# Last group of a fused normalise-MLP-modulate kernel: variance by token, last product chunk by chunk, and the orders of groups 0 and 1 redone

## What is computed

```python
# x: 8 x 1024 tokens of 512 features
h = LN(LN(x, pw_g[id], pw_b[id]), cp_g[kind], cp_b[kind])   # two layer norms, rows looked up by token
t = LN(x, tm_g[kind], tm_b[kind]);  s = LN(x, ms_g[scale], ms_b[scale])
m, n, r = (x + LN(silu(c @ W1 + b1) @ W2 + b2) for each of three conditions)   # one row per batch
w = softmax(aw)
cat = [w0*h, w1*t, w2*m, w3*n, w4*r, w5*s]
u = silu(cat @ int_W1 + int_b1) @ int_W2 + int_b2
x1 = x + (u - mean(u)) / sqrt(var(u) + EPS) * int_g + int_be
style = cond @ (affine_w / 16).T + affine_b
dcoef = 1 / sqrt(sum((weight * style)**2) + 1e-8)
out = x1 + clip(((x1 * style) @ weight.T) * dcoef + bias, -256, 256)
```

## Time and profile before

| | us |
|---|---|
| runs | 1206.86 median of 3 (1206.23 to 1208.74) |
| the profiled execution's own time | 1205.75 |
| its span, first to last instruction | 1204.0 |
| PE, DVE, ACT, POOL busy | 1168.7, 945.9, 548.6, 228.5 |
| mean granted TensorE clock | 0.994 of full speed |

### The profile page before, as it was taken

How to read it: one execution, slowest core, us unless ns; L and a number is a source line. 1 busy time by engine, 2 the same in 40 slices (tenths; PEclk the granted TensorE clock), 3 DMA queues, 4 the chain that set the end, 5 groups by cost and what they waited for, 6 DMA issues and landing times.

```text
span 1204.0 us, 15227 instructions
## 1 busy us (share of the span) xinstructions
PE 1168.7 (97%) x5268; PEld 947.9 (79%) x5268; DVE 945.9 (79%) x1755; ACT 548.6 (46%) x849; POOL 228.5 (19%) x268
## 2 busy tenths in 40 slices
PE   5899899999999999999999999999999999999996
PEld 3567688888888888888888888888888888888884
DVE  7897887968788786878878688797878879687736
ACT  3546244453634446363453635345363444536352
POOL 3521211202121121112103111210212112021000
PEclk9999899999999999999999999999999999999998
DMA  9941231412333142233313223231323314122001
GB/s 320 347 159 42 70 121 43 142 59 88 103 97 120 36 140 69 79 112 96 112 35 124 77 86 121 70 131 42 105 86 97 120 43 142 60 88 88 27 1 69
DMA packets 52011, 119.50 MB, mean 99 GB/s; under 512 B 6464, under 2 KB 6848, under 8 KB 51840
## 3 DMA queue, kind: packets, MB, share of 16 engines
q1 hardware_dynamic: 36512, 67.58, 17.7%
q0 software_dynamic: 14336, 50.34, 12.7%
q10 hardware_dynamic: 1088, 0.62, 0.2%
HBM read 101.74 MB, written 16.78 MB: 98 GB/s over the span
## 4 chain that ended last, share of the span: by engine, by line
PE 91%; DVE 4%; DMA 2%; issue 1%; SPq 1%; POOL 1%; ACT 1%; DVEq 0%; ACTq 0%
PE pre L1152 14%; PE pre L1156 13%; PE pre L1159 13%; PE pre L1190 5%; PE pre L1192 5%; PE pre L1191 5%; PE uy L1210 5%; PE uy L1211 5%; PE uy L1213 5%; PE uy L1226 5%; PE uy L1223 5%; PE uy L1224 5%; PE turn L1131 2%; PE turn L1115 2%; DMA early_hi_l<-affine_t 2%; PE pre L1173 1%
## 5 line engine op out<-in xcount | busy, mean ns | idle before, releaser
L369 POOL DMA_INDIRECT gb<-pw_table,pw_ids x63 | 66.3, 1053 | 332.6 <-PE turn L1115 317.8
L1223 PE MATMUL uy<-hi_a,w_hi_l 128*128 128x512 f32 x256 | 100.5, 392 | 4.7 <-ACT hi_a L532 4.7
L1210 PE MATMUL uy<-hi_c,w_hi_w 128*128 128x512 f32 x256 | 101.4, 396 | 0.0
L1226 PE MATMUL uy<-lo_a,w_hi_l 128*128 128x512 f32 x256 | 100.6, 393 | 0.7 <-DVE lo_a L848 0.7
L1224 PE MATMUL uy<-hi_a,w_lo_l 128*128 128x512 f32 x256 | 100.3, 392 | 0.0
L1211 PE MATMUL uy<-hi_c,w_lo_w 128*128 128x512 f32 x256 | 100.0, 391 | 0.0
L1213 PE MATMUL uy<-lo_c,w_hi_w 128*128 128x512 f32 x256 | 99.9, 390 | 0.0
L1190 PE MATMUL pre<-hi_b,w_hi_x 128*128 128x512 f32 x256 | 99.8, 390 | 0.0
L1192 PE MATMUL pre<-lo_b,w_hi_x 128*128 128x512 f32 x256 | 99.7, 389 | 0.0
L1191 PE MATMUL pre<-hi_b,w_lo_x 128*128 128x512 f32 x256 | 99.6, 389 | 0.0
L387 POOL TENSOR_TENSOR ra<-vea,half 128x1 f32<-128x1 f32 x64 | 42.5, 664 | 281.3 <-DVE vea L745 281.3
(11 more groups left out here) (218 smaller groups left out, 2893.7 us busy)
## 6 DMA issues: line engine op xcount, KB each, us to landing
xT<-x_turned SPq DMA_DIRECT2D x64, 256.0 KB, 2.8
out_turned<-xT SPq DMA_DIRECT2D x64, 256.0 KB, 2.1
xt<-x_in SPq DMA_DIRECT2D x62, 256.0 KB, 2.6
sel_in<-sel_ids SPq DMA_DIRECT2D x16, 192.0 KB, 2.4
raw_s<-int_w SPq DMA_DIRECT2D x2, 512.0 KB
raw_h<-int_w SPq DMA_DIRECT2D x1, 1024.0 KB, 23.2
early_hi_w<-mlp_w SPq DMA_DIRECT2D x1, 1024.0 KB, 19.8
raw_w<-mlp_w SPq DMA_DIRECT2D x1, 1024.0 KB, 22.0
```

What stands on the lines that cost most here:

```text
L1210: pe.matmul(bank, w_hi["w2"][:, c, cut], hi["c"][:, c, :], start=c == 0, stop=False)
L1223: pe.matmul(bank, w_hi["l1"][:, c, cut], hi["a"][:, c, :], start=c == 0, stop=False)
L1226: last = pe.matmul(bank, w_hi["l1"][:, c, cut], lo["a"][:, c, :], start=False, stop=c == C - 1)
```

## The change

Four things change.

1. **Last group, root.** `last_variance` takes the sum over partitions with the squares as weights and a single column of 1/512 as moving operand: four matmuls in plain float32, one for each 128 tokens, with 128 x 1 results. DVE copies the 128 x 4 numbers, POOL takes the power, DVE writes four diagonal matrices (`last_diag`), and `spread_root`, one float32 matmul, spreads them to 128 x 512 in `turn`, where `make_x1` reads them. `split_sum`, `low_sum`, `read_var` and `find_root` are gone for group 15.
2. **Last group, product.** `last_y` writes to the four banks `pre` and goes chunk by chunk: outputs 0, 1, 2 together, then output 3. Its operands lie in ring c. Each `split_x1` of ACT comes between the `y_out` of group 14, and three `finish` of group 14 come behind `all_x1(15)`.
3. **Group 1.** The lo part of l1 is made by DVE in four chunks around group 1's first `low_t`, the hi part by ACT in four chunks around `hidden(0, 3)`; POOL's operation is gone. `find_root(0)` moves behind `second_norm(7)`.
4. **Group 0.** On ACT `split_h(0, 1)` comes ahead of the h weights, `gate(3)` and `split_h(0, 3)` ahead of all four `split_x`. POOL does `rstd_a(2)` and `rstd_a(3)` ahead of the h weights and the power `c_rs` between them, not behind four gathers. DVE takes `first_norm(2)` ahead of `make_s(0, 3)`, `second_norm(2)` ahead of the MLP's copy, all `low_h` ahead of all `low_x`, and the scaling `cT_ready` ahead of the second part of `wsum`; the softmax pieces are interleaved differently.

```diff
+    return uses + [("var", GROUPS - 1), ("root", GROUPS - 1)]
...
             rstd_a(1)
+            rstd_a(2)
+            rstd_a(3)
             low_h_weights(0)
             low_h_weights(1)
-            rstd_a(2)
+            pool.wait_ge(c_var, 1)
+            nc.gpsimd.tensor_tensor(crow[0:TROWS, 3:4], crow[0:TROWS, 2:3], half[0:TROWS, :], ALU.pow).then_inc(c_rs, 1)
             low_h_weights(2)
             low_h_weights(3)
-            rstd_a(3)
...
+            pool.wait_ge(var_read, GROUPS)
+            nc.gpsimd.tensor_tensor(last_root, last_var, half[:].to_broadcast([P, TPG]), ALU.pow).then_inc(last_rstd, 1)
...
             hidden(0, 2)
             filled(act, "batch")
             nc.scalar.activation(mh, filled(act, "dsum"), ACT.Copy).then_inc(dsum_copied, 1)
+            for c in range(2):
+                nc.scalar.activation(w_hi["l1"][:, c, :], raw_w["l1"][:, c, :], ACT.Copy).then_inc(hi_done["l1"], 1)
             hidden(0, 3)
+            for c in range(2, C):
+                nc.scalar.activation(w_hi["l1"][:, c, :], raw_w["l1"][:, c, :], ACT.Copy).then_inc(hi_done["l1"], 1)
...
             u_out(i, 3)
-            split_sum(i)
             y_out(i - 1, 0)
             y_out(i - 1, 1)
-            read_var(i)
+            split_x1(i, 0)
+            split_x1(i, 1)
             y_out(i - 1, 2)
+            split_x1(i, 2)
             y_out(i - 1, 3)
-            for c in range(C):
-                split_x1(i, c)
+            split_x1(i, 3)
...
             low_h(0, 2)
-            low_x(0, 0)
-            low_x(0, 1)
+            low_h(0, 3)
+            dve.wait_ge(style_ready, 1)
+            style4 = style[:].unsqueeze(2).to_broadcast([P, C, 4, BATCH])
+            nc.vector.tensor_tensor(sstyle.rearrange("p c (r b) -> p c r b", b=BATCH), style4, style4, ALU.mult).then_inc(style_ready, 1)
             dve.wait_ge(mlp2_mm, 1)
...
-            low_h(0, 3)
-            low_x(0, 2)
-            low_x(0, 3)
+            for c in range(C):
+                low_x(0, c)
             dve.wait_ge(c_rs, 1)
...
             make_t(1, 0)
+            low("l1", 0, 1.0)
             low_t(1, 0)
+            low("l1", 1, 1.0)
             add_square(0, 1)
...
+            bank = filled(dve, "var", i)
+            nc.vector.tensor_copy(last_var, bank[:, 0:TPG]).then_inc(var_read, 1)
             finish(i - 1, 0)
-            find_root(i)
-            finish(i - 1, 1)
+            dve.wait_ge(last_rstd, 1)
+            nc.vector.scalar_tensor_tensor(out=last_diag, in0=ident.unsqueeze(1).to_broadcast([P, TPG, P]), scalar=float(D),
+                                           in1=last_root.unsqueeze(2).to_broadcast([P, TPG, P]), op0=ALU.mult,
+                                           op1=ALU.mult).then_inc(last_scaled, 1)
             all_x1(i)
...
+            def last_variance():
+                bank = fill("var", GROUPS - 1)
+                pe.wait_ge(sq_added, 3 * GROUPS)
+                for j in range(TPG):
+                    last = pe.matmul(bank[:, j:j + 1], sq0[:, j * P:(j + 1) * P], vmat[:, 0:1].bitcast(F32), start=True, stop=True)
+                last.then_inc(turn_filled, 1)
...
             unit_y(i - 1, 0)
-            variance(i)
-            for o in range(1, C):
-                unit_y(i - 1, o)
-            for o in range(C):
-                unit_y(i, o)
+            last_variance()
+            unit_y(i - 1, 1)
+            spread_root()
+            unit_y(i - 1, 2)
+            unit_y(i - 1, 3)
+            pe.wait_ge(hid_raw, GROUPS * C)
+            last_y((0, 1, 2))
+            last_y((3,))
```

More of the change, by code:

```diff
@@ L554, in _ @@
             table_high("t")
-            act.wait_ge(aw_ready, 1)
+            split_rows(0)
+            act.wait_ge(aw_ready, 2)
             high("t", 0, wsm[:, 1:2])
-            split_rows(0)
             high("t", 1, wsm[:, 1:2])
@@ L589, in _ @@
             gate(2)
+            gate(3)
             split_h(0, 2)
+            split_h(0, 3)
             split_x(0, 0)
             split_x(0, 1)
-            gate(3)
-            split_h(0, 3)
             split_x(0, 2)
@@ L839, in make_x1 @@
                 dve.wait_ge(uy_read, u_use(i, c) + 1)
-                dve.wait_ge(root_ready, i + 1)
-                nc.vector.tensor_tensor(ug[:, c, :], ug[:, c, :], root[:], ALU.mult).then_inc(xq_done, 1)
+                if i + 1 < GROUPS:
+                    dve.wait_ge(root_ready, i + 1)
+                    rstd = root[:]
+                else:
+                    rstd = filled(dve, "root", i)
+                nc.vector.tensor_tensor(ug[:, c, :], ug[:, c, :], rstd, ALU.mult).then_inc(xq_done, 1)
                 dve.wait_ge(xq_done, i * C + c + 1)
@@ L890, in _ @@
             low_rows(0)
+            dve.wait_ge(aw_ready, 2)
             make_t(0, 0)
@@ L919, in _ @@
             low_h(0, 0)
-            make_s(0, 3)
             low("s", 2, wsm[:, 5:6])
             low_s(0, 2)
+            first_norm(2)
+            make_s(0, 3)
             low("s", 3, wsm[:, 5:6])
             low_s(0, 3)
-            first_norm(2)
+            second_norm(2)
             bank = filled(dve, "mlp_h").rearrange("p (c r) -> p c r", c=C)
@@ L1012, in _ @@
             make_t(1, 0)
+            low("l1", 0, 1.0)
             low_t(1, 0)
+            low("l1", 1, 1.0)
             add_square(0, 1)
             make_t(1, 1)
+            low("l1", 2, 1.0)
             low_t(1, 1)
@@ L1020, in _ @@
             make_t(1, 2)
+            low("l1", 3, 1.0)
             for i in range(1, GROUPS):
@@ L1041, in _ @@
                     dve.wait_ge(dco_ready, 1)
-                find_root(i - 1)
+                else:
+                    find_root(i - 1)
                 low_h(i, 1)
@@ L1049, in _ @@
                 second_norm(f - 1)
+                if i == 1:
+                    find_root(0)
                 low_h(i, 3)
@@ L1227, in unit_y, with spread_root, last_y @@
                 last.then_inc(y_ready, 1)
+            def last_variance():
[4 more added lines that the diff above has]
+                last.then_inc(turn_filled, 1)
+            def spread_root():
+                bank = fill("root", GROUPS - 1)
+                pe.wait_ge(last_scaled, 1)
+                pe.matmul(bank, vmat[:, 0:1].bitcast(F32).to_broadcast([P, P]), last_diag.rearrange("p j t -> p (j t)"),
+                          start=True, stop=True).then_inc(turn_filled, 1)
+            def last_y(outs):
+                i = GROUPS - 1
+                ring = x1_ring(i)
+                for c in range(C):
+                    pe.wait_ge(x1_hi, i * C + c + 1)
+                    for o in outs:
+                        pe.matmul(pre[:, o, :], w_hi["l1"][:, c, o * P:(o + 1) * P], hi[ring][:, c, :], start=c == 0, stop=False)
+                    for o in outs:
+                        pe.matmul(pre[:, o, :], w_lo["l1"][:, c, o * P:(o + 1) * P], hi[ring][:, c, :], start=False, stop=False)
+                    pe.wait_ge(x1_lo, i * C + c + 1)
+                    for o in outs:
+                        last = pe.matmul(pre[:, o, :], w_hi["l1"][:, c, o * P:(o + 1) * P], lo[ring][:, c, :], start=False, stop=c == C - 1)
+                        if c == C - 1:
+                            last.then_inc(y_ready, 1)
             def mlp_first():
```

67 lines of the change are left out of this document (30 added, 37 removed).

## The result

The changed kernel takes 1192.03 us, the median of 4 runs (1191.81 to 1192.47), beside 1206.55 (1204.79 to 1208.74) for the kernel before on the same chip: a ratio of 0.9877 with a 95% interval of 0.9861 to 0.9893. The forecast was 1192.1. The profiled execution took 1191.81, its span is 1189.7 against 1204.0.

The account below looks back on a forecast made before the run. PE, busy 97% of the span, was taken to bound the kernel, with DVE pacing part of group 0. End -7.8, group 1 -7.2, group 0 +0.2: -14.8 on the median 1206.86 gave 1192.1, range 1189.2 to 1196.0.

Parts of the forecast that it names:

- The end, -7.8 forecast: From `unit_y(14)` to the program's end: PE never waits, last matmul starts at 1191.2 against 1199.05; with 0.1 allowed, -7.8 us.
- The price of one column: End, `last_variance`: four float32 matmuls with one moving column take 0.81 us, as with 32 columns; bounds 0 and 3.4.
- The slack at `spread_root`: End: copy, power and DVE work of about 2.2 us fit into 2.7 us, half a microsecond of slack at best.
- The backlog of 0.1: Behind the last matmul: `y_out` and `finish` of outputs 0 to 2 come due together; 0.1 us allowed.
- Group 1, -7.2 forecast: Group 1: removing the 4.98 us stall and low clock's 2.6, less a 0.4 PE wait, gains 7.2 us.
- l1's parts on DVE at 0: Group 1: four new lo parts, 2.6 us on DVE, cost 0 because DVE waited there for ACT; uncovered, 2.6.
- Group 0, +0.2 forecast: Group 0: DVE's last three operations up to `c_ready` start 0.6 later, an idle 0.41 downstream goes; group's end +0.2 us.
- the full 0.90 for each of the two: Group 0: DVE loses 0.90 us beside each of two `low_h_weights` and 0.56 for POOL's small table, 2.36 in all.
- the upper bound of +1.5: Group 0: DVE waits for POOL's whole 3.10 and 0.56 us, moving the group's end by +1.5.
- the 2.4 us of group 0 that cost no clock: Group 0's old gate wait, cited in the late root rival as a pause as long as its 2.5 us.
- the rival of the late root: End: root's chain 3 us late, `spread_root` holds PE 2.5 us: 1194.6; chance 0.13, of which 0.03 at 1199.
- the time above the one before that had a chance of 0.02: Whole kernel: the case that the change makes it slower than before; chance 0.02.

Follow-up runs that it names:

- e3: Kernel before with only the change's new orders of group 0: 1206.39 us, ratio 0.9989 to the kernel before.
- e2: Kernel before with only the change's group 1 (l1's lo part on DVE, `find_root(0)` moved): 1199.81 us, ratio 0.9919.
- e7: Changed kernel with `find_root(0)` back in its old place, l1's lo part still on DVE: 1192.61 us, ratio 0.9881.
- e8: Changed kernel with l1's lo part back on POOL, `find_root(0)` in its new place: 1192.87 us, ratio 0.9882.
- e12: Changed kernel with one more, unused DVE operation ahead of each of the four lo parts of l1: 1193.14 us.
- e4: The changed kernel unaltered, run again beside the single parts: 1193.33 us, ratio 0.9861 to the kernel before.
- e11: The changed kernel unaltered, run again in a later call: 1192.25 us, ratio 0.9873 to the kernel before.
- e1: Kernel before with only the change's end (last group's root and product): 1197.30 us, ratio 0.9899.
- e9: Changed kernel with all of group 0 in its old order: 1191.66 us, ratio 0.986 to the kernel before.
- e5: Changed kernel with POOL's h weights and small table all ahead of the wait for `c_var`, then the power: 1190.01 us, ratio 0.9862.
- e10: The kernel of e5 run once more, in the same call as e11: 1188.85 us, ratio 0.984.

## Why the prediction was right, point by point

- **The end, -7.8 forecast, -7.70 measured.** The mechanism is as forecast. The price of one column, taken from the row of 32 columns, was exact: 0.81. The eight weight loads of the four matmuls take 1.08 with one column in the changed kernel (from 1163.93) and 1.09 with 32 columns in the kernel before (from 79.55). `spread_root` was 0.86, exact too. The rest is a pace of (23.39 - 1.67) / 95 = 0.229 us a matmul for the 0.226 that I read. The slack at `spread_root`, said to be half a microsecond at best, is 0.58. The backlog of 0.1 behind the last matmul is not there. The -7.70 holds against the trace of before; against the old ends of e3 and e2 it would be 1 to 2 us more.
- **Group 1, -7.2 forecast, -7.29 measured.** PE's wait at the lo matmuls is 0.17 instead of 0.4. What I hadn't seen is that the two edits overlap: e7 and e8 show that each removes most of the stall, so that they are no sum of two terms.
- **l1's parts on DVE at 0.** Right, and the traces show it apart: from `gain(t, 1, 0)` to the s gain that stood at 121.31, behind all four parts, PE takes 121.31 - 95.19 = 26.12 before, 26.08 in the changed kernel, and 122.64 - 96.50 = 26.14 in e8, where the parts are back on POOL. In e12 it is 27.04: of what was put in on top, 2.7, the cover takes 1.8 and 0.9 is left to pay.
- **Group 0, +0.2 forecast, +0.69 measured: the step that failed.** The prediction took "the full 0.90 for each of the two" `low_h_weights` and "0.56 again for the table", and had `low_x` stretched to 1.5 each. Both are wrong. POOL's power stands ahead of the weights in POOL's order and was itself held until the four `low_x` were through, so the weights never ran beside the `low_x`. Those weren't touched, and what they were to lose fell on one operation behind them: 3.72 - 0.60 = 3.12 for the 2.36 of the sum. The last operation up to `c_ready`, before and after:

```profile
60.71 0.69 DVE L953 TENSOR_TENSOR sq<-sq,xT 96x512 f32<-96x512 f32 x1
...
61.77 0.69 DVE L966 TENSOR_TENSOR sq<-sq,xT 96x512 f32<-96x512 f32 x1
```

  `c_ready` moved from 61.40 to 62.46, +1.06 where I had +0.6. From there to the gain row it is 33.42 for 33.79, about the idle 0.41 that I had taken out. PE's transpose did not move back: it stood at 63.35 before and stands at 62.61.

  The +0.69 is too small by luck. In all seven traces with the new orders and POOL's order of the changed kernel (after, e3, e4, e7, e8, e11, e12) the gain row comes 49.6 behind the start of `mlp_second`, and that start was 46.28 where the trace of before has 47.01. With the start of before the gain row would stand at 96.6: +1.4, about the upper bound of +1.5.

  The fault was to read the 0.43 and 0.90 of the earlier trace rows as a price for each pair of operations. There DVE and POOL took turns: POOL's two operations last 1.43 and 1.72, the second from 47.83, and each DVE operation was held only by what was left of the one POOL operation already begun. In the changed kernel DVE was let in only after all three.

  Which DVE operations POOL held up is shown one by one. Held up were the first of e8's two `lo_b`, with both operands in SBUF (1.63, where the second takes 0.68), and also two that read one SBUF tensor each, the operation of 3.72 and the integer step of the earlier trace rows, 4.74. Not held up was e8's operation of 0.69, with one operand in PSUM. So two operands in SBUF are not what all of them share; what decides it, no run shows.
- **The clock.** The prediction used "the 2.4 us of group 0 that cost no clock" as evidence that a pause so long is harmless. It held in the profiled execution of before, and e1, e2 and e9 show a fall behind pauses of 2.7 to 2.9. Behind the 1.9 us wait at the transpose the clock fell in e3, e4, e8 and e11 (0.56, 0.50, 0.61 and 0.50 in the lowest 3 us), and not in the changed kernel, e7 and e12. In these seven it cost nothing: the gain row comes 49.6 behind `mlp_second` with the fall and without, since DVE sets the pace there (busy for 31.91 to 31.98 of the 33.80 us from 61.30 to 95.10). So the clock is no rival for the gain of e5 and e10 either. The forecast didn't rest on it, but the rival of the late root did. At the end PE sets the pace, so 1194.6 may have been too mild a price for a pause of 2.5; no run tests it. Nor does a run show the time above the one before that had a chance of 0.02: where the clock fell behind the transpose, its mean from 61.30 to 95.10 was still 0.95 (e3, e4, e8, e11).
- **The total.** -14.8 against the profiled execution; it measured -14.3 in span and -14.5 in medians. In the two profiled executions the misses (+0.1 at the end, -0.1 in group 1, +0.5 in group 0) add up to 0.5. The median lies 0.1 from the forecast, and that closeness is partly luck: group 0 would have missed by 1.2 with the start of `mlp_second` as before, and that start moves the time about one for one (45.93, 46.28 and 48.58 in e11, the changed kernel and e4, whose profiled executions took 1191.26, 1191.81 and 1194.03). What carries the prediction are its two large terms.

## What to carry to other kernels

When DVE operations of the kinds held up here stand beside POOL's, count as the upper bound POOL's whole unbroken queue against the next DVE operation (3.72 for 0.60 here), and DVE's against POOL's (2.73 for the power's 0.59); one turn of the other engine is the lower one, as in the earlier trace rows (1.17 and 1.64 for 0.74). A POOL operation that someone waits for (here a power of one column) belongs at the end of such a queue, with the bulk work ahead of it in time that nobody needs: here two lines moved, 2.6 to 3.4 us and the fastest version of the study (1188.85). And before adding up two remedies for one stall, ask whether either alone removes it.

## What the runs showed of the hardware that was new to me

DVE and POOL did not meet only at semaphores: in the cases below no semaphore stands between the operation that was held up and those that held it. Unbroken runs of operations were mostly not interleaved: DVE's four `low_x` of 2.48 us held off a POOL power until they were through (2.73), and POOL's three operations of 3.5 us held off one DVE operation that asked 0.06 us after the first had begun (3.72), and about the same in e3, e4, e7, e8, e11 and e12. In the earlier trace rows a pair of POOL operations and two DVE operations did alternate: POOL's pair took 3.10 where it takes 2.50 alone (from 47.92 in the changed kernel). What decides between the two is open.

The clock fell behind pauses of nearly one length in some executions and not in others: after 2.4 in before it was at 1.00, after 1.9 at the transpose 1.00 in the changed kernel and 0.50 in e4 and e11. A term that puts no clock cost on a wait of this length should carry a bound for it.
